# Running ranks kept in TensorE's bank, a third phase copy on VectorE, and the first lists in idle buffers

## The chip, the cores and the metric

The kernel runs on one core of one Trainium2 chip. The metric is the device time of one execution in microseconds (us), lower is better. The core has five engines with a queue each: TensorE (PE, with its weight loads shown as PEld), VectorE (DVE), ScalarE (ACT), GpSimd (POOL) and SyncE (SP, which only issues DMAs here). They run side by side and wait for each other through semaphores.

## The reference, cut to what matters

x is (128 samples, 32 channels, 512). Two layers are added onto it. The change is in the first:

```python
# layer 0: grouped conv (9 taps, 4 groups) + context, then a top-2 mixture of 8 experts
h = conv(x, weight) + (c @ c_weight.T)[:, :, None] + bias[None, :, None]
logits = h @ W_gate + b_gate                   # (128, 32, 8)
_, top_idx = top_k(logits, 2)
y_all = relu(einsum('bsd,edh->bseh', h, W_e) + b_e)
x = x + take_along_axis(y_all, top_idx[..., None], axis=2).mean(axis=2)
# layer 1: attention over 8 kernels mixes channels, then a linear layer with 4-bit weights
x = x + (einsum('boi,bih->boh', agg_w, x) + agg_b) @ dequantized_W.T + bias
```

There are 4096 tokens (sample, channel) of 512 values. The kernel doesn't compute all eight experts for each token. It sorts the tokens into lists, one region of a DRAM tensor per expert, and multiplies each list by its expert's matrix only.

## The kernel before, in words

Three stages follow each other. The order in each engine's queue is written out by hand; a step index g, s or g again runs through each stage, and every engine has its own `step1`, `step2`, `step3`.

**Stage 1** (32 steps, one per group of 4 samples, 128 tokens). For group g:
- SP has loaded x into one of four buffers `xt`. `split_phase` (L365) copies one of four phases (every fourth element) of it into a quarter of the partitions of `phases`. VectorE makes phases 0 and 1 (`split_x`, L699), ScalarE phases 2 and 3 (L573 to L578), for group g+2 while TensorE works on g+1.
- TensorE convolves (L1185 to L1190, 12 matmuls in float32, 24 records). ScalarE copies the result to `hT` (L568).
- `gate_and_rows` (L1163), one step later: four matmuls give partial gate logits and transposed rows. VectorE reduces the logits and finds the two best experts (L832 to L872); ScalarE writes the token rows to `token_list` (L596).
- `count_ranks` (L1156), two steps later: `before` (ones for every earlier token) times `chosen` gives each token's rank inside the group, `ones` times `chosen` the count per expert. VectorE adds the running offset `base` (L838), keeps `base` up to date (L848), and picks the row of each of the token's two experts (L854, L863). POOL scatters the token's row to `lists_d` twice (L522).
- In steps 16 to 26 VectorE also computes, from the counts of the first 15 groups, the table of the first eight list tiles (`early_table`, 19 instructions).
- ScalarE issues the four loads of the experts' biases `be_bc` (L603), 512 KB each, in steps 18 to 21. In steps 24 to 29 a small network for layer 1 (`mix_layers`, `mix_softmax`) is computed in between.

Steps 4 to 15 are a hardware loop (`Fori`), where waits are on computed register values; the others are written out.

**Stage 2** (71 list tiles, 128 tokens each). SP loads tile a of `lists_d` into `xt` in four DMAs and its keys in a fifth (L432, L435); before tiles 0 to 3 it waits until all 32 groups have been split out of `xt` (L424 to L426). VectorE transposes it into `lT` (`transpose_list`, L935), TensorE multiplies it by the expert's weights (`product`, L1204, four matmuls of 512 columns), VectorE adds the bias (L953), ScalarE applies the ReLU, POOL scatters the result. Tiles 0 to 3 are transposed by VectorE between its last steps of stage 1 (L961 to L969). Tiles 8 and up need the final table, which VectorE computes from the final counts (L984 to L1007) and TensorE spreads (L1248 to L1250) after product 4.

**Stage 3** (32 groups): the pairs are summed with x, mixed, and multiplied by the 4-bit matrix.

On TensorE the passage from stage 1 to 2 reads: convolution 31, ranks 29, gate 30, gate 31, product 0, ranks 30, product 1, ranks 31, three matmuls of the mixing kernels (L1150 to L1154), product 2.

## Time and profile before

| | |
|---|---|
| three runs | 516.99 us median (516.94 to 518.96) |
| the profiled execution | 518.35 us, its span 516.6 us |
| PE busy | 491.2 us (95% of the span) |
| PEld, DVE | 321.6 us (62%), 345.6 us (67%) |
| ACT, POOL | 197.6 us (38%), 157.5 us (30%) |
| mean granted TensorE clock | 0.981 of full speed |

Busy shares are means over three stages with different limits. The rows further down are read by stretch: a stretch belongs to stage 1 up to about 142 us, to stage 2 from about 152 to 395 us, to stage 3 from there. Times in a timeline row are the start in us and the duration in us; what stands in brackets is the idle time of the engine before the row and who ended it. A row with xN merges N like instructions.

### The profile page before, as it was taken

To read this page: it belongs to the slowest core of one execution; us is meant where nothing else is said; L and a number is where in the kernel's file an instruction comes from. 1 tells how busy PE (TensorE), PEld (TensorE's weight loads), DVE (VectorE), ACT (ScalarE), POOL (GpSimd) and SP (SyncE) were. 2 spreads that over 40 slices of the span, in tenths; PEclk is the share of its full clock that TensorE was granted. 3 is DMA by queue.
4 is the path that set the end of the run, shared out by engine and by line. 5 is a ranking of instruction groups with operands and counts; after the bars stand their busy time and mean duration, and the time that the engine had idled before them with its cause. 6 is when DMAs were issued, how large, how long until landed. Compare 5 with 4: busy or idle time off the path is not lost. (4 is left out here: it accounts for less than half of the span.)

```text
span 516.6 us, 10152 instructions
## 1 busy us (share of the span) xinstructions
PE 491.2 (95%) x2284; PEld 321.6 (62%) x2285; DVE 345.6 (67%) x1087; ACT 197.6 (38%) x341; POOL 157.5 (30%) x178
## 2 busy tenths in 40 slices
PE   5999999999869999999999999999997999999996
PEld 5999999989844443444444444444544777777674
DVE  6877888877546657573354435453445799999996
ACT  6798999999721111111111111111222222222220
POOL 9154555444435522233323332333224000000000
PEclk9999999999969999999999999999997999999998
DMA  6569878998467686676666657575554688889852
GB/s 182 142 233 298 285 241 269 361 374 269 154 165 188 209 228 168 165 201 181 174 187 163 183 150 197 163 191 146 155 143 169 245 292 292 277 292 287 286 184 102
DMA packets 90050, 110.94 MB, mean 215 GB/s; under 512 B 25198, under 2 KB 61726, under 8 KB 88980
## 3 DMA queue, kind: packets, MB, share of 16 engines
q1 hardware_dynamic: 71808, 69.14, 47.1%
q0 software_dynamic: 11664, 36.24, 19.7%
q10 hardware_dynamic: 6536, 5.09, 3.3%
q8 instruction: 15, 0.25, 0.2%
q14 instruction: 27, 0.22, 0.2%
HBM read 65.44 MB, written 46.51 MB: 217 GB/s over the span
## 5 line engine op out<-in xcount | busy, mean ns | idle before, releaser
L1213 PE MATMUL bank<-we,lT 128*128 x536 | 233.7, 597 | 0.7 <-DVE ring_a L953 0.7
L1213 PEld LDWEIGHTS bank<-we,lT 128*128 128x128 f32 x536 | 101.8, 191 | 128.1 <-issue 127.9
L539 POOL DMA_INDIRECT pairs_d<-ring_b,pair_i x71 | 71.0, 999 | 161.0 <-DVE pair_i L942 109.2
L630 ACT ACTIVATE ring_b<-ring_a 128x512 f32<-128x512 f32 x71 | 44.7, 630 | 196.3 <-DVE ring_a L953 188.2
L953 DVE TENSOR_TENSOR ring_a<-bank,be_bc 128x512 f32<-128x512 f32 x71 | 49.0, 691 | 101.8 <-PE bank L1213 92.4
L1187 PE MATMUL bank<-wconv,phases 128*128 128x128 f32 x768 | 93.8, 280 | 1.2 <-ACT phases L367 1.2
L522 POOL DMA_INDIRECT lists_d<-token_list,row_i x64 | 66.7, 1042 | 83.3 <-ACT token_list L596 57.1
L1187 PEld LDWEIGHTS bank<-wconv,phases 128*128 128x128 f32 x768 | 90.8, 196 | 1.4 <-ACT phases L367 1.4
L367 ACT COPY phases<-xt 32x512 f32<-32x512 f32 x64 | 71.4, 1116 | 1.2
L939 DVE STREAM_TRANSPOSE lT<-xt 128x512 f32<-128x512 f32 x71 | 49.9, 703 | 11.1 <-DMA keys<-lists_d 10.8
L367 DVE COPY phases<-xt 32x512 f32<-32x512 f32 x64 | 44.7, 698 | 10.2 <-PE bank L1187 8.5
L1174 PE MATMUL bank<-wg,lT 128*128 128x136 f32 x256 | 39.2, 298 | 4.1 <-ACT token_list L596 3.7
L1280 PE MATMUL bank<-wq,high 128*128 128x512 f32 x128 | 38.8, 426 | 3.5 <-PEq L1228 3.5
L1174 PEld LDWEIGHTS bank<-wg,lT 128*128 128x128 f32 x256 | 33.5, 198 | 5.2 <-issue 4.5
L1284 PE MATMUL bank<-wq,low 128*128 128x512 f32 x128 | 35.9, 403 | 0.0
L1259 PE MATMUL bank<-mix_bd,we 128*128 128x128 f32 x224 | 32.0, 286 | 0.0
L685 ACT CAST high<-bank 128x512 fp32r<-128x512 f32 x32 | 18.7, 586 | 34.2 <-PE bank L1259 34.2
L596 ACT ACTIVATE token_list<-bank,ctx_col 128x256 f32<-128x256 f32 x64 | 26.8, 469 | 10.9 <-DVE partial L832 9.9
L1259 PEld LDWEIGHTS bank<-mix_bd,we 128*128 128x128 f32 x224 | 27.4, 191 | 4.6 <-DVE we L1066 4.3
L1284 PEld LDWEIGHTS bank<-wq,low 128*128 128x128 f32 x128 | 24.6, 192 | 6.0
L1280 PEld LDWEIGHTS bank<-wq,high 128*128 128x128 f32 x128 | 22.7, 197 | 7.3 <-issue 4.3
L678 ACT CAST rows_r<-bank 34x128 fp32r<-34x128 f32 x32 | 8.3, 258 | 48.5 <-PE bank L1266 48.5
(196 smaller groups left out, 384.3 us busy)
## 6 DMA issues: line engine op xcount, KB each, us to landing
xt<-lists_d SPq DMA_DIRECT2D x284, 64.0 KB, 2.1
xt<-in_x SPq DMA_DIRECT2D x60, 256.0 KB, 3.9
we<-pairs_d SPq DMA_DIRECT2D x28, 512.0 KB, 4.8
we<-in_L_ffn_W_e SPq DMA_DIRECT2D x8, 1024.0 KB, 6.5
out<-orow_list SPq DMA_DIRECT2D x32, 256.0 KB, 2.8
lists_d<-orow_list SPq DMA_DIRECT2D x8, 257.0 KB
be_bc<-in_L_ffn_b_e ACTq DMA_DIRECT2D x4, 512.0 KB, 9.5
words<-pairs_d POOLq DMA_DIRECT2D x4, 512.0 KB, 5.3
```

The source lines that it names most:

```text
L367: return copy(phases[q * C:(q + 1) * C, jb, :, 1:P + 1], x_quad[jq].rearrange("c s (l q) -> c q s l", q=PH)[:, q, :, :])
L522: pool.indirect_dma_start(lists_d, bass.IndirectOffsetOnAxis(ap=row_i[:, j, k:k + 1], axis=0), token_list[:, j, :], None, bounds_check=E * ...
L539: pool.indirect_dma_start(pairs_d, bass.IndirectOffsetOnAxis(ap=pair_i[:, s % DR:s % DR + 1], axis=0), ring_b[:, s % U, :], None, bounds_c ...
L630: act.activation(ring_b[:, j, :], ring_a[:, j % 2, :], ACT.Relu, scale=0.5).then_inc(result_ready, 1)
L939: dve.transpose(lT[:, ja, :].rearrange("m (p h r) -> m h p r", p=PH, h=MH), xt[:, ja, :].rearrange("r (h p l) -> r h p l", h=MH, p=PH)).th ...
L953: dve.tensor_tensor(ring_a[:, j % 2, :], ps_exp[j % 2][:, :], be_bc[:, bass.ds(expert, 1), :].rearrange("p a n -> p (a n)"), ALU.add).then ...
L1174: mm = pe.matmul(ps_both[:, p // 2, cols], hT[:, ja % 2, p * P:(p + 1) * P], wg[:, p, :], start=True, stop=True)
L1187: mm = pe.matmul(ps_conv[j % 2][:, s * P:(s + 1) * P], phases[:, j % 2, s, t:t + P], wconv[:, t, :, :].rearrange("k p o -> k (p o)"), star ...
L1213: mm = pe.matmul(ps_exp[j % 2][:, :], lT[:, j, p * P:(p + 1) * P], we[:, bass.ds(expert, 1), p, :].rearrange("m a n -> m (a n)"), start=(p ...
L1259: mm = pe.matmul(ps_mix[a % 2][:, q * P:(q + 1) * P], y_of(a)[:, q * P:(q + 1) * P], mix_bd[:, a, :], start=True, stop=True)
L1280: pe.matmul(ps_lin[j][:, :], high[:, j % 2, q * P:(q + 1) * P], wq[:, q, :], start=(q == 0), stop=False, skip_group_check=True)
L1284: mm = pe.matmul(ps_lin[j][:, :], low[:, j % 2, q * P:(q + 1) * P], wq[:, q, :], start=False, stop=(q == PH - 1), skip_group_check=True)
```

## The change

- **Ranks.** `count_ranks` no longer restarts its bank. Before the first group, a matmul of one row puts the regions' first rows into columns 0 to 7 and zeros into 8 to 15. In each later group one more matmul (`others` times the chosen of the group before; `others` is the complement of `before`) completes the last group's contribution, so columns 0 to 7 always hold the running row number. VectorE reads it straight: `rank` and `base` additions go; the two picking instructions become one product over 2 x 8 and one reduction; the mask of both experts is made at once. VectorE's small instructions of a step go from 12 to 10. TensorE now waits until the rank of the group before was read (`picked_ready`).
- **Phases.** VectorE copies phase 2 as well (`split_third`), at the end of its step; ScalarE copies only phase 3.
- **Lists 0 to 3** are loaded into `ring_a` 0 and 1 and `ring_b` 2 and 3, idle in stage 1, with no wait for the splits. That wait now stands ahead of list 4, which also waits for the transpose of list 0.
- **Biases** are loaded in steps 0 to 3 of stage 1.
- **Order on TensorE.** 4 warm-up transposes ahead of the 12 transposes of the convolution's weights and 8 behind them; the three matmuls of the mixing kernels move ahead of gate 31.
- POOL makes `others` and `rank_init` before its other constants (four more instructions in place of one).

```diff
         ring_b = sb("ring_b", [P, U, L])
+        first_list = [ring_a[:, 0, :], ring_a[:, 1, :], ring_b[:, 2, :], ring_b[:, 3, :]]
...
+        def list_of(a, ja):
+
+            return first_list[a] if isinstance(a, int) and a < len(first_list) else xt[:, ja, :]
...
-                    if isinstance(a, int) and a < XR:
+                    if isinstance(a, int) and a == XR:
                         sp.wait_ge(act_split, NG)
                         sp.wait_ge(dve_split, NG)
-                    else:
+                    if not isinstance(a, int) or a >= XR:
                         wait(sp, lT_ready, a - XR + 1)
                         wait(sp, pair_ready, a - XR + 1)
 
                     for mh in range(MH):
-                        sp.dma_start(xt[mh * B:(mh + 1) * B, ja, :].rearrange("r (h n) -> r h n", h=MH),
+                        sp.dma_start(list_of(a, ja)[mh * B:(mh + 1) * B, :].rearrange("r (h n) -> r h n", h=MH),
...
+            pool.memset(others[:, :], 1.0).then_inc(others_one, 1)
+            pool.wait_ge(others_one, 1)
+            pool.affine_select(out=others[:, :], in_=others[:, :], compare_op=ALU.is_ge, fill=0.0, base=0,
+                               pattern=[[-1, P]], channel_multiplier=1).then_inc(consts, 1)
             exact = dict(allow_small_or_imprecise_dtypes=True)
             pool.iota(iota_e[:, :], pattern=[[1, E]], base=0, channel_multiplier=0, **exact).then_inc(consts, 1)
             pool.iota(region[:, :], pattern=[[REGION, E]], base=P, channel_multiplier=0, **exact).then_inc(consts, 1)
-            pool.iota(base[:, :], pattern=[[REGION, E]], base=P, channel_multiplier=0, **exact).then_inc(consts, 1)
+            pool.iota(rank_init[:, 0:E], pattern=[[REGION, E]], base=P, channel_multiplier=0, **exact).then_inc(consts, 1)
+            pool.memset(rank_init[:, E:], 0.0).then_inc(consts, 1)
...
-                    for q in range(PH // 2, PH):
-                        ins = split_phase(act.copy, q, ja, j % 2)
-                    ins.then_inc(act_split, 1)
+                    split_phase(act.copy, 3, ja, j % 2).then_inc(act_split, 1)
...
-                if isinstance(g, int) and hi1 + 2 <= g < hi1 + 6:
-                    e = slice((g - hi1 - 2) * 2, (g - hi1 - 2) * 2 + 2)
+                if isinstance(g, int) and 0 <= g < 4:
+                    e = slice(2 * g, 2 * g + 2)
                     act.dma_start(be_bc[:, e, :].rearrange("p e n -> p (e n)"),
                                   b_e[e].rearrange("(a e) n -> a (e n)", a=1).to_broadcast((P, 2 * L))).then_inc(be_in, 16)
...
-                for q in range(PH // 2):
-                    ins = split_phase(dve.tensor_copy, q, ja, ja % 2)
-                ins.then_inc(dve_split, 1)
+                split_phase(dve.tensor_copy, 0, ja, ja % 2)
+                split_phase(dve.tensor_copy, 1, ja, ja % 2)
+
+            def split_third(ja):
+
+                split_phase(dve.tensor_copy, 2, ja, ja % 2).then_inc(dve_split, 1)
             dve.memset(wfull[:, :, :], 0.0).then_inc(wfull_zero, 1)
             dve.wait_ge(convw_in, 16 * (C // CG))
             pick_taps(dve.tensor_copy, range(PH // 2), dve_taps)
             split_x(0, 0)
+            split_third(0)
             for t in range(SHIFTS):
                 dve.wait_ge(wT_done, t + 1)
                 dve.tensor_copy(wconv[:, t, :, :].rearrange("k p o -> k (p o)"), ps_w[t][:, 0:P]).then_inc(wconv_ready, 1)
...
                 deq_step(dve.scalar_tensor_tensor(terms_w[:, :], full_low, odd[0:RK, 0:1], full, ALU.mult, ALU.add))
             split_x(1, 1)
+            split_third(1)
             dve.wait_ge(consts, N_CONSTS)
             def context_columns():
...
                 if live(b, NG):
                     wait(dve, rank_done, b + 1)
-                    wait(dve, base_ready, b)
-                    dve.tensor_tensor(rank[:, :], ps_rank[:, 0:E], base[:, :], ALU.add).then_inc(rank_ready, 1)
+                    dve.tensor_tensor(picked[:, :, :], masks[:, :, :],
+                                      ps_rank[:, 0:E].rearrange("p (a e) -> p a e", a=1).to_broadcast((P, 2, E)), ALU.mult).then_inc(picked_ready, 1)
                 if live(a, NG):
                     wait(dve, partial_ready, a + 1)
                     if isinstance(g, int) and a == 0:
                         dve.wait_ge(gbias_ready, 2)
                     dve.tensor_tensor(logit[:, :], partial[:, :], gate_bias[:, bass.ds(a, 1), :].rearrange("p a e -> p (a e)"), ALU.add).then_inc(logit_ready, 1)
+                if live(b, NG):
+
+                    wait(dve, picked_ready, b + 1)
                 if live(a, NG):
                     wait(dve, logit_ready, a + 1)
                 if live(b, NG):
-                    wait(dve, rank_ready, b + 1)
-                    dve.tensor_tensor(base[:, :], base[:, :], ps_rank[:, E:2 * E], ALU.add).then_inc(base_ready, 1)
+                    dve.tensor_reduce(row_of[:, :], picked[:, :, :], AX.X, ALU.add).then_inc(row_ready, 1)
                 if live(a, NG):
                     dve.max(top[:, :], logit[:, :]).then_inc(top_ready, 1)
                     wait(dve, top_ready, a + 1)
                 if live(b, NG):
-                    for k in range(2):
-                        dve.scalar_tensor_tensor(picked[:, k, :], iota_e[:, :], expert_of[:, bass.ds(b, 1), 1 + k:2 + k].rearrange("p a k -> p (a k)"),
-                                                 rank[:, :], ALU.is_equal, ALU.mult,
-                                                 accum_out=row_of[:, bass.ds(b, 1), k:k + 1].rearrange("p a k -> p (a k)")).then_inc(row_ready, 1)
+                    wait(dve, row_ready, b + 1)
+                    wait(dve, scattered[jb], (b - jb) * (32 // U))
+                    dve.tensor_scalar(row_i[:, jb, :], row_of[:, :], 0.0, None, ALU.add).then_inc(rowi_ready, 1)
                 if live(a, NG):
                     dve.max_index(topi[:, :], top[:, :], logit[:, :]).then_inc(topi_ready, 1)
-                if live(b, NG):
-
-                    wait(dve, row_ready, 2 * b + 2)
-                    wait(dve, scattered[jb], (b - jb) * (32 // U))
-                    dve.tensor_scalar(row_i[:, jb, :], row_of[:, bass.ds(b, 1), :].rearrange("p a k -> p (a k)"), 0.0, None, ALU.add).then_inc(rowi_ready, 1)
-                if live(a, NG):
                     wait(dve, topi_ready, a + 1)
                     dve.tensor_scalar(expert_of[:, bass.ds(a, 1), 1:3].rearrange("p a k -> p (a k)"), topi[:, 0:2], 0.0, None, ALU.add).then_inc(expert_ready, 1)
                     wait(dve, expert_ready, a + 1)
-                    e1, e2 = (expert_of[:, bass.ds(a, 1), 1 + k:2 + k].rearrange("p a k -> p (a k)") for k in range(2))
-                    dve.tensor_scalar(chosen1[:, :], iota_e[:, :], e1, None, ALU.is_equal).then_inc(chosen1_ready, 1)
-                    wait(dve, chosen1_ready, a + 1)
+                    dve.tensor_tensor(masks[:, :, :], iota_e[:, :].rearrange("p (a e) -> p a e", a=1).to_broadcast((P, 2, E)),
+                                      expert_of[:, bass.ds(a, 1), 1:3].rearrange("p a k -> p k a").to_broadcast((P, 2, E)), ALU.is_equal).then_inc(masks_ready, 1)
+                    wait(dve, masks_ready, a + 1)
                     wait(dve, rank_done, a - 3)
-                    dve.scalar_tensor_tensor(chosen[:, ja, :], iota_e[:, :], e2, chosen1[:, :], ALU.is_equal, ALU.add).then_inc(chosen_ready, 1)
+                    dve.tensor_tensor(chosen[:, ja, :], masks[:, 0, :], masks[:, 1, :], ALU.add).then_inc(chosen_ready, 1)
+                if live(g + 2, NG):
+                    split_third((j + 2) % U)
...
-                    dve.wait_ge(base_ready, counted)
-                    early_op(dve.tensor_tensor(tint[:, :], base[:, :], region[:, :], ALU.subtract))
+                    dve.wait_ge(rank_done, counted)
+                    early_op(dve.tensor_scalar(tint[:, :], ps_rank[:, E:2 * E], 0.0, None, ALU.add))
...
+            warm_up(WARM_START // 2)
             for t in range(SHIFTS):
                 pe.wait_ge(dve_taps, t + 1)
                 pe.wait_ge(act_taps, t + 1)
                     mm = pe.transpose(ps_w[t][:, p * C:(p + 1) * C],
                                       wsel[:, t * PH + p, :, :].rearrange("o q i -> o (q i)"), ident[0:C, 0:C])
                 mm.then_inc(wT_done, 1)
+            warm_up(WARM_START)
             def context_products():
...
             def count_ranks(a, ja):
                 wait(pe, chosen_ready, a + 1)
-                wait(pe, base_ready, a)
-                pe.matmul(ps_rank[:, 0:E], before[:, :], chosen[:, ja, :], start=True, stop=True)
-                pe.matmul(ps_rank[:, E:2 * E], ones[:, :], chosen[:, ja, :], start=True, stop=True).then_inc(rank_done, 1)
+                wait(pe, picked_ready, a)
+                if isinstance(a, int) and a == counted:
+                    pe.wait_ge(early, 1)
+                if isinstance(a, int) and a == 0:
+                    pe.wait_ge(consts, N_CONSTS)
+                    pe.matmul(ps_rank[:, 0:2 * E], one_row[0:1, 0:1].to_broadcast((1, P)), rank_init[:, :], start=True, stop=False, skip_group_check=True)
+                else:
+                    pe.matmul(ps_rank[:, 0:E], others[:, :], chosen[:, (ja - 1) % U, :], start=False, stop=False, skip_group_check=True)
+                pe.matmul(ps_rank[:, 0:E], before[:, :], chosen[:, ja, :], start=False, stop=False, skip_group_check=True)
+                pe.matmul(ps_rank[:, E:2 * E], ones[:, :], chosen[:, ja, :], start=False, stop=True, skip_group_check=True).then_inc(rank_done, 1)
             def gate_and_rows(a, ja):
...
                         mm = pe.matmul(ps_low[0][0:RK, :], ones_r[:, :], wq[:, q, :], start=(q == 0), stop=(q == 3))
                     mm.then_inc(colsum_done, 1)
+            mix_layers(NG + 1 - mlp_first)
             gate_and_rows(NG - 1, (NG - 1) % U)
             pe.wait_ge(early, N_EARLY)
             pe.wait_ge(we_in, 16 * E)
...
             count_ranks(NG - 2, (NG - 2) % U)
             product(1, 1)
             count_ranks(NG - 1, (NG - 1) % U)
-            mix_layers(NG + 1 - mlp_first)
             for s in range(2, 5):
                 product(s, s % U)
             pe.wait_ge(tab_ready, 1)
```

## Rows read from the trace of the kernel before

**Rows 1.** Busy time by stretch: us, then PE, PEld, DVE, ACT, POOL; clock, DMA.
```profile
80.00:120.00 40.00, 38.21 (x337) 37.45 (x337) 32.41 (x184) 37.57 (x59) 20.50 (x20) 1.00 0.95 330
200.00:400.00 200.00, 196.46 (x476) 89.52 (x475) 98.98 (x207) 38.21 (x62) 61.87 (x64) 0.99 0.63 171
```

**Rows 2.** The page's costliest groups: ScalarE's phase copies (busy us, mean ns | idle).
```profile
L367 ACT COPY phases<-xt 32x512 f32<-32x512 f32 x64 | 71.4, 1116 | 1.2
```

**Rows 3.** Timeline of PE: convolutions 1, 4, 16, 17, 27, 30, gate 29, convolution 31.
```profile
16.29 2.92 PE L1187 MATMUL bank<-wconv,phases 128*128 128x128 f32 x24
...
27.86 2.84 PE L1187 MATMUL bank<-wconv,phases 128*128 128x128 f32 x24
...
77.19 2.84 PE L1187 MATMUL bank<-wconv,phases 128*128 128x128 f32 x24
...
81.12 2.84 PE L1187 MATMUL bank<-wconv,phases 128*128 128x128 f32 x24
...
122.83 2.92 PE L1187 MATMUL bank<-wconv,phases 128*128 128x128 f32 x24
...
136.22 2.84 PE L1187 MATMUL bank<-wconv,phases 128*128 128x128 f32 x24
...
138.95 1.17 PE L1174 MATMUL bank<-wg,lT 128*128 128x136 f32 x8
139.96 2.84 PE L1187 MATMUL bank<-wconv,phases 128*128 128x128 f32 x24
```

**Rows 4.** Timeline of VectorE: a step in the loop, one written out.
```profile
64.17 1.24 DVE L367 COPY phases<-xt 32x512 f32<-32x512 f32 x2 [0.44 <-PE bank L1187]
...
67.84 0.23 DVE L872 SCALAR_TENSOR_TENSOR chosen<-iota_e,expert_of,chosen 128x8 bf16<-128x8 f32 x1 [0.15 <-DVE chosen L869]
...
133.03 0.19 DVE L832 TENSOR_REDUCE partial<-bank 128x8 f32<-128x32 f32 x1
...
134.83 0.23 DVE L872 SCALAR_TENSOR_TENSOR chosen<-iota_e,expert_of,chosen 128x8 bf16<-128x8 f32 x1
```

**Rows 5.** Timeline at the start: a VectorE copy and the POOL memset beside it.
```profile
9.98 5.49 DVE L367 COPY phases<-xt 32x512 f32<-32x512 f32 x1
...
11.59 3.53 POOL L513 MEMSET mix_bd<- 128x4096 f32 x1
```

**Rows 6.** Timeline: a scatter's issue on POOL; two small VectorE instructions of the table.
```profile
63.87 1.04 POOL L522 DMA_INDIRECT lists_d<-token_list,row_i  x1 [1.72 <-ACT token_list L596]
...
167.37 1.27 DVE L995 TENSOR_SCALAR prefix<-late_n,block_at 128x8 f32<-128x8 f32 x1
...
170.27 0.16 DVE L1006 TENSOR_TENSOR tab_f<-row_at,used 128x1 f32<-128x1 f32 x1
```

**Rows 7.** SyncE's waits, its first list load, and VectorE's first list transpose.
```profile
SPq L426 <- DVE phases L367: 10.1, 1, 10.1
...
137.88 1.88 SPq L432 DMA_DIRECT2D xt<-lists_d  x4
...
143.78 0.71 DVE L939 STREAM_TRANSPOSE lT<-xt 128x512 f32<-128x512 f32 x1 [5.18 <-DMA keys<-lists_d]
```

**Rows 8.** Timeline of PE between stage 1 and 2, up to the table's transpose.
```profile
146.53 0.19 PE L1160 MATMUL bank<-chosen,before 128*128 128x8 bf16 x1 [3.73 <-DVE chosen L872]
...
150.10 2.15 PE L1174 MATMUL bank<-wg,lT 128*128 128x136 f32 x8 [1.32 <-ACT token_list L596]
152.04 5.29 PE L1213 MATMUL bank<-we,lT 128*128 x8
...
160.87 1.98 PE L1153 MATMUL bank<-ring_b,attT 8*128 8x512 f32 x4
...
162.92 10.57 PE L1213 MATMUL bank<-we,lT 128*128 x24
173.32 0.27 PE L1249 MATMUL bank<-ident,tab_f 128*3 128x128 f32 x1
```

**Rows 9.** PE by stretch: us, busy, granted clock, DMA share, GB/s.
```profile
152.00:154.00 2.00, 2.00 (x5) 0.50 0.76 222
```

22 lines of the change are left out of this document (12 added, 10 removed).

## The prediction

> **What bounds the kernel now.** I read the busy tenths and the windows by stretch first, then PE's timeline, then the waits of PE, VectorE and SyncE around what the change touches. In stage 2 PE alone sets the pace: it is busy 196.46 of 200 us, no other engine over 100 [rows 1]. In stage 1 PE and ScalarE are both near full, 38.2 and 37.6 of 40 us, VectorE has 32.4 [rows 1]. The reader is to see in [rows 3] that the convolutions start 4.11 us apart in the loop ((77.19 - 27.86) / 12), 4.15 us apart in steps 16 to 27 ((122.83 - 77.19) / 11) and 4.28 us apart to step 31. Where PE waits for nothing a step takes 3.93 us in the loop (77.19 to 81.12) and 3.74 us written out (136.22 to 139.96). Between the stages PE stands still for 3.73 and 1.32 us [rows 8] behind VectorE, which stood 5.18 us in its own queue for list 0 [rows 7]. Its clock had fallen by then: the granted clock is 0.50 (1.2 GHz) at 152 us [rows 9], after the idle 3.73 us, and gates 30 and 31 take 2.15 us each [rows 8] where gate 29 took 1.17 [rows 3], product 0 takes 5.3 us. What PE loses before product 2 arrives at the end one for one, as the rest of stage 2 is PE's.
>
> **Part 1, lists 0 to 3 and the order on TensorE.** SP waited 10.1 us for the splits before it issued list 0 at 137.88 [rows 7], so it was ready at 127.8. After, the eight tiles' table (done with step 26) is its last wait, and one list takes it some 3 us to issue and land (137.88 to 143.78 held the wait and the landing). List 0 is there by about 134, VectorE asks for it at about 138.6 (143.78 - 5.18): the stall goes. What is late next? List 3 is issued last, at about 137, 10 us ahead of its transpose. List 4 now waits for the splits, over by 137.8, and for list 0's transpose, so it goes out no later than it did.
> Without the stall the passage is PE's own work from convolution 31 (139.96) to product 2. At the full clock: convolution 2.68, gate 30 1.0 (138.95 to 139.96 [rows 3]), mixing kernels 2.05 (160.87 to 162.92 [rows 8]), gate 31 1.0, two products of 3.5 (10.57 / 3 [rows 8]), three counts of 0.1: 14.0 us. The mixing kernels now lie between gate 30 and 31, where PE otherwise waits about 1.2 us for ScalarE to empty gate 30's bank; they cost nothing new and cover that. Before, the same passage took 162.92 - 139.96 = 22.96. Gain 22.96 - 14.0 = 9.0; I take 8.9. Its parts: waits 5.05, the clock about 3.9 (gates 2 x 1.0, product 0 1.8). If a new wait of 3 us lets the clock fall again, the gain is 5; 9.5 is the most.
> Behind it: the final table. VectorE had it at 170.43 [rows 6], PE wanted it at 173.32 [rows 8], 2.9 us later, but 2.05 us of PE's work have moved ahead of that chain, and the POOL memset that held VectorE's instruction for 1.27 us [rows 6] comes along with the scatters. About 0.8 us is left; down to 0 and a wait of 1.5 us is in the range.
>
> **Part 2, VectorE in stage 1.** A split of two phases takes 1.24 us [rows 4], so a third adds 0.62, and I take 0.65 with its own start. The small instructions run from 65.41, the end of the copies, to 68.07 in the loop, 2.66 us for 12 (0.22 each), and from 133.03 to 135.06, 2.03 us (0.17 each), written out [rows 4]. Ten of them: 2.2 and 1.7 us. A step of VectorE is then 1.24 + 0.65 + 2.2 = 4.1 us in the loop (3.9 before) and 3.6 written out (3.3). The new forms (2 x 8 products with a PSUM operand, the reduction) aren't in the trace; taken at the spacing of those of 8 columns, at worst they save nothing (loop 4.5, written out 3.9), at best 0.15 more than said.
>
> **Part 3, ScalarE in stage 1.** It loses a copy of 1.12 us in each step [rows 2] and goes from about 3.9 to 2.8 us. So it stops pacing stage 1, and its two late table loads and the network's activations, which make steps 24 to 29 long now, fall into slack. Next in line is VectorE where it is over PE's floor, else PE.
>
> **Part 4, TensorE in stage 1.** One more bf16 matmul with 8 columns per group. From convolution 30's start to gate 29's are 2.73 us [rows 3] with the two counts in between, and 24 records of a convolution alone take 2.68 (2.84 less the end of the last one), so the two take 0.05 to 0.1. I take 0.04 for the third, floor 3.97 and 3.78; 0.1 is the upper end. The wait on `picked_ready` is met a step ahead, as VectorE reads the ranks first after the gate's reduction. Before count 15 PE waits once for the early table's first instruction, which stands behind step 16's third copy: 0 to 0.6 us.
>
> **The sum for stage 1.**
> - Loop, 12 steps: from 4.11 to 4.10, as VectorE paces: -0.1 (from -1.7 at PE's floor to +5 if the small instructions save nothing).
> - Steps 16 to 27: VectorE 11 x 3.6 = 39.9, and the early table's 19 instructions of 0.17 add 3.2: 43.1, PE's floor 42.4 with the network's matmuls; against 45.64: -2.3 (-3.5 to 0).
> - Steps 27 to 31: 17.13 now; four VectorE steps of 3.6 and some 1.9 us for the softmax with its wait for ScalarE: 16.4, so -0.7 (-1.5 to +0.5).
> - Start: a VectorE copy that began at 9.98 ended only at 15.47, when POOL's memset (11.59 to 15.12) was over [rows 5], and convolution 1 followed at 16.29. Now two copies stand behind that point in place of one (+0.65), and POOL's four instructions for one shift the memset by 0.5: +1.1. Convolution 0 may run earlier or at the full clock thanks to the 12 warm-up transposes, but then waits for the same copy. From -0.5 to +3.5 (the clock falls while PE waits some 3 us for it).
> Together -2.0.
>
> **The biases.** Four 0.5 MB loads leave steps 18 to 21, where the DMA engines are 0.95 busy [rows 1], for steps 0 to 3. x is loaded four steps ahead, and the third copy frees its buffer about 3 us later of 16, so neither makes a split wait. Nothing for the cost; the relief is inside the -2.3.
>
> **A rule that speaks against the change.** POOL issues a scatter for 1.04 us from 63.87, and two VectorE copies that start inside it, at 64.17, take their usual 1.24 us [rows 4, 6]; beside the memset a copy took 5.49 us [rows 5]. The Trainium skill (SBUF — State Buffer, on the shared port pair) has it that VectorE's fast fp32 SBUF-to-SBUF copy and GpSimd exclude each other for a whole instruction, descriptor writing included. The memsets agree with that rule, the scatters here don't.
>
> **The rivals.**
> - A, the stage 1 terms come to nothing or cost: the loop at 4.35 (+3), the start +2, and steps 16 to 31 only -2. Then 516.99 - 8.9 + 3 = 511. For: VectorE is close to being the bound. Chance 0.14.
> - B, stage 1 falls to PE's floor throughout: -1.7, -3.3, -1.5, start 0, that is -6.5 and 501.6. For: the small forms carry fewer waits. Against: the third copy alone fills VectorE's slack. Chance 0.12.
> - C, the passage gives less: a wait for the table or a fallen clock, 4 us less: 510. Chance 0.12.
> - D, slower: the third copy, at the end of VectorE's step and beside both scatters' issues, is held by them for 1.0 us each step. VectorE's step is 5.1 in the loop and 4.9 behind it: 12 x 1.0 + 15 x 0.8 + 1 = +25, less 8.9: 533. It decides from 0.4 us of hold per step (28 x 0.4 = 11). Against: [rows 4, 6]. By the skill's rule this is what would happen. Chance 0.04.
> - E, the change does not do what it says: list 0 is still late, since SP reaches it late. Then only stage 1 counts: 515. Against: SP's 10.1 us. Chance 0.03.
>
> **How the numbers follow.** The sum is -8.9 - 2.0 = -10.9, on a profiled execution of 518.35 us (span 516.6, 1.75 around it): 507.4. The median of the runs is 516.99, 1.36 less than the profiled one, so 506.1; I forecast 506.2, chance 0.55. A, B, and C lie inside 501.5 to 511.5, where I leave out D, E and the ends. 0.5% of 517 is 2.6 us, about what a measurement can tell from no change: faster by that means below 514.4. Faster 0.93, within 0.03, slower 0.04.
>
> **What would show it.** VectorE has no idle time for the keys of list 0, PE's largest wait for `chosen` is under 1 us, the clock stays at 1.00 from 140 to 160 us, and product 2 starts at about 152. ScalarE is busy about 28 of 40 us in 80 to 120, VectorE 37. Convolutions start 4.1 us apart in the loop and 3.9 behind it; convolution 1 starts at about 17.4. Wrong would be: VectorE's copies longer than 0.7 us each beside scatters, a new PE wait at the table's matmul, or stage 2 running slower than 3.4 us a tile.

## The result, and the profile after

The kernel after takes 509.11 us (median of 4 runs, 508.53 to 511.47), the kernel before 517.19 on the same chip (516.94 to 518.96): a ratio of 0.9845, 95% interval 0.9807 to 0.9883. That is 8.1 us faster, where 10.9 were forecast; inside the range. The profiled execution took 509.02 us (span 507.3), against 518.35, so the two traces differ by 9.3 us.

Busy time by stretch in the kernel after; the columns are those of [rows 1], which it answers.

```profile
80.00:120.00 40.00, 38.92 (x357) 38.12 (x356) 35.73 (x155) 28.98 (x54) 24.35 (x21) 1.00 0.89 285
200.00:400.00 200.00, 196.46 (x502) 92.88 (x502) 98.08 (x204) 39.88 (x67) 61.00 (x62) 0.98 0.63 175
```

ScalarE fell from 37.57 to 28.98 of 40 us, VectorE rose from 32.41 to 35.73, and PE rose to 38.92: in stage 1 it is now PE that is full. Stage 2 is what it was. The phase copies, from the costliest groups [rows 2]: VectorE makes 96 in place of 64, ScalarE 32.

```profile
L373 DVE COPY phases<-xt 32x512 f32<-32x512 f32 x96 | 64.1, 667 | 2.7 <-PE bank L1207 0.4
...
L373 ACT COPY phases<-xt 32x512 f32<-32x512 f32 x32 | 35.9, 1122 | 0.8
```

PE's timeline, convolution 1, then 16 and 17 [rows 3]: they start 3.90 us apart, (76.78 - 29.61) / 12 = 3.93 over the loop from convolution 4.

```profile
17.77 2.92 PE L1207 MATMUL bank<-wconv,phases 128*128 128x128 f32 x24
...
76.78 2.84 PE L1207 MATMUL bank<-wconv,phases 128*128 128x128 f32 x24
...
80.68 2.84 PE L1207 MATMUL bank<-wconv,phases 128*128 128x128 f32 x24
```

PE's timeline between the stages [rows 8]. It has no long gap any more: 0.49 us before gate 31, and the gates take 1.17, product 0 takes 3.69 us (2.15 and 5.29 before). The granted clock is 1.00 throughout 140 to 160 us, the 2.4 GHz level, where [rows 9] had 0.50. New are the waits of 0.75 us, at product 5 behind the table's transpose, and of 0.56.

```profile
140.45 1.17 PE L1194 MATMUL bank<-wg,lT 128*128 128x136 f32 x8
141.55 1.98 PE L1166 MATMUL bank<-ring_b,attT 8*128 8x512 f32 x4
...
144.16 1.16 PE L1194 MATMUL bank<-wg,lT 128*128 128x136 f32 x8 [0.49 <-ACT token_list L605]
145.27 3.69 PE L1233 MATMUL bank<-we,lT 128*128 x8
...
152.57 10.56 PE L1233 MATMUL bank<-we,lT 128*128 x24
162.97 0.27 PE L1269 MATMUL bank<-ident,tab_f 128*3 128x128 f32 x1
...
164.21 10.56 PE L1233 MATMUL bank<-we,lT 128*128 x24 [0.75 <-DVE ring_a L964]
```

SyncE issues the four lists from 125.93 us on [rows 7] (shown: the first and the last); VectorE finds list 0 landed.

```profile
125.93 2.05 SPq L438 DMA_DIRECT2D ring_a<-lists_d  x4
...
137.01 1.97 SPq L438 DMA_DIRECT2D ring_b<-lists_d  x4
```

For the experiments I use one ledger, from PE's timelines of the profiled executions. "Start" is the start of convolution 4, "loop" 4 to 16, then 16 to 27 and 27 to 31, "passage" convolution 31 to product 2, "rest" from there to the end of the span. The medians come from 4 or more runs each.

```
                        start   loop  16-27  27-31  passage   rest    median
before                  27.86  49.33  45.64  17.13   22.96  353.68   517.19
after                   29.61  47.17  44.00  16.91   14.88  354.73   509.11
lists alone             27.79  49.14  45.08  17.12   17.92  352.85   512.10
lists and order         27.79  49.09  45.39  17.13   14.30  353.80   510.37
after without lists     28.47  47.19  43.99  16.91   24.44  353.20   516.20
before with filler      27.79  49.10  45.81  17.12   20.25  355.53   514.64
third copy on ScalarE   28.50  47.77  44.71  17.03   14.13  353.16   507.97
matrix memset first     29.05  47.17  44.04  16.89   16.36  355.29   510.91
no warm-ups             29.18  47.16  43.99  16.93   14.86  355.08   509.77
rows' memset late       29.19  47.23  43.96  16.93   14.79  352.50   508.45
both memsets late       28.36  47.19  44.03  16.89   14.13  352.80   506.13
biases late             28.62  47.14  44.64  16.35   14.14  354.31   508.46
both late, third on ACT 26.30  48.32  44.71  17.00   14.13  353.44   507.97
the same, gap filled    26.71  47.90  44.75  17.00   14.13  353.31   508.79
```

One median lies within some 1 us of where another four runs would put it, since runs of one kernel spread by 2 to 5 us; differences of stretches are much sharper. The kernel before was run again beside the experiments, with medians of 517.12 (beside the first four kernels below "after"), 518.38 (third copy on ScalarE, matrix memset first, no warm-ups, rows' memset late) and 517.98 (the other four), so medians of different sets carry up to 1.3 us of that too; each ratio below is against the kernel before.

### The profile page after: what moved, and what is told of

The parts are those of the page before. It is cut to its first block and busy times, and to the rows that moved or that the text cites. A ratio compares the mean times of both kernels' runs of the same rounds, so it can differ in the third digit from the quotient of the medians.

```text
span 507.3 us, 10035 instructions
## 1 busy us (share of the span) xinstructions
PE 489.4 (96%) x2329; PEld 320.8 (63%) x2330; DVE 352.1 (69%) x992; ACT 164.7 (32%) x309; POOL 165.4 (33%) x181
## 5 line engine op out<-in xcount | busy, mean ns | idle before, releaser
L533 POOL DMA_INDIRECT lists_d<-token_list,row_i x64 | 73.4, 1147 | 67.5 <-ACT token_list L605 46.6
L373 DVE COPY phases<-xt 32x512 f32<-32x512 f32 x96 | 64.1, 667 | 2.7 <-PE bank L1207 0.4
L950 DVE STREAM_TRANSPOSE lT<-xt 128x512 f32<-128x512 f32 x67 | 47.0, 701 | 8.8 <-DMA keys<-lists_d 8.3
L1194 PE MATMUL bank<-wg,lT 128*128 128x136 f32 x256 | 37.3, 288 | 0.5 <-ACT token_list L605 0.5
L373 ACT COPY phases<-xt 32x512 f32<-32x512 f32 x32 | 35.9, 1122 | 0.8
L1194 PEld LDWEIGHTS bank<-wg,lT 128*128 128x128 f32 x256 | 31.8, 190 | 0.7 <-issue 0.6
L579 ACT COPY lT<-bank 128x512 f32<-128x512 f32 x32 | 18.7, 585 | 35.8 <-PE bank L1207 35.8
```

Source lines behind the costliest of these rows:

```text
L373: return copy(phases[q * C:(q + 1) * C, jb, :, 1:P + 1], x_quad[jq].rearrange("c s (l q) -> c q s l", q=PH)[:, q, :, :])
L533: pool.indirect_dma_start(lists_d, bass.IndirectOffsetOnAxis(ap=row_i[:, j, k:k + 1], axis=0), token_list[:, j, :], None, bounds_check=E * ...
L950: dve.transpose(lT[:, ja, :].rearrange("m (p h r) -> m h p r", p=PH, h=MH), list_of(a, ja).rearrange("r (h p l) -> r h p l", h=MH, p=PH)). ...
L1194: mm = pe.matmul(ps_both[:, p // 2, cols], hT[:, ja % 2, p * P:(p + 1) * P], wg[:, p, :], start=True, stop=True)
```

## Experiments: the lists, the order and the clock

**Lists alone.** The kernel before with lists 0 to 3 in the idle buffers and nothing else.

```diff
+        first_list = [ring_a[:, 0, :], ring_a[:, 1, :], ring_b[:, 2, :], ring_b[:, 3, :]]
...
-                    if isinstance(a, int) and a < XR:
+                    if isinstance(a, int) and a == XR:
```

> The kernel before with nothing but lists 0 to 3 in the idle buffers and their wait moved to list 4. Theory 'the stall of VectorE for list 0 cost the passage': convolution 31 starts near 140 as before, VectorE doesn't wait for list 0, the granted clock stays at 1.00, convolution 31 to product 2 takes 15.2 us (14.0 and the 1.2 that PE waits for ScalarE at gate 31) in place of 22.96: 7.7 us less, 509.5. Rival 'list 0 is late for another reason (SyncE reaches it late, or the transfer)': the stall stays, under 2 us less, 515 to 517. Rival 'the gain came from ranks and the third copy': no change.

512.10 us, ratio 0.9896 (0.9861 to 0.9932). PE's timeline of this kernel:

```profile
144.35 1.17 PE L1179 MATMUL bank<-wg,lT 128*128 128x136 f32 x8 [1.32 <-ACT token_list L601]
146.08 5.39 PE L1218 MATMUL bank<-we,lT 128*128 x8 [0.57 <-DVE lT L944]
```

And its busy time by stretch (us; PE, PEld, DVE, ACT, POOL; granted clock, DMA share, GB/s):

```profile
144.00:146.00 2.00, 1.17 (x8) 0.99 (x8) 1.86 (x13) 0.43 (x3) 0.59 (x1) 1.00 0.75 232
146.00:148.00 2.00, 1.92 (x3) 0.94 (x4) 0.00 (x0) 0.81 (x2) 1.38 (x2) 0.59 0.70 197
148.00:150.00 2.00, 2.00 (x3) 0.71 (x3) 0.00 (x0) 0.00 (x0) 0.00 (x0) 0.56 0.76 215
```

The 5.18 us stall is gone, yet PE still idles 1.32 and 0.57 us; right after it the granted clock falls towards 0.50 (1.2 GHz) and product 0 takes 5.39 us in place of 3.69. So the clock is not saved by removing the big stall alone. The expectation's 15.2 us for the passage, with the clock at 1.00, was missed by 2.7.

**Lists and order.** The same, with the mixing matmuls between gates 30 and 31.

```diff
             count_ranks(NG - 1, (NG - 1) % U)
-            mix_layers(NG + 1 - mlp_first)
...
+            mix_layers(NG + 1 - mlp_first)
             gate_and_rows(NG - 1, (NG - 1) % U)
```

> As the run with the lists alone, and the three matmuls of the mixing kernels ahead of gate 31. If they cover PE's wait for ScalarE there: 14.9 us from convolution 31 to product 2 (what the changed kernel takes), 0.3 to 1.2 us less than with the lists alone, 508.5 to 509.2. Rival 'they only push the final table's chain onto PE's path': the passage is shorter but PE waits for VectorE at product 5 by as much, and the time is that of the lists alone.

510.37 us, 0.9865 (0.9827 to 0.9902); passage 14.30, 3.6 us less than with the lists alone. The move does two things: it covers idle time, 1.89 us of it with the 0.57 behind gate 31, and with that keeps the clock (1.00 from 140 to 162 us; product 0 takes 3.60 us for 5.39). By the medians it is worth only 1.7 us, and the expected 508.5 to 509.2 was missed: "rest" grew by 0.95, and PE, which had no wait at product 5 with the lists alone, now waits 0.48 us there. So the rival in the expectation, the table's chain pushed onto PE's path, holds in part. Both small edits together give the kernel before 6.8 of the 8.1 us by the medians.

**After without the lists.** Everything of the change but the lists' buffers (the reverse of the first diff).

> The changed kernel with lists 0 to 3 in xt and the wait for the splits ahead of list 0, as before. All of stage 1's parts stay. Theory: convolution 31 starts at 137.7 (2.3 us less than before), then the stall is back, with list 0 issued some 3 us later than before since phase 2 is copied at the end of VectorE's step: 24 to 26 us from convolution 31 to product 2 or less by the 1 us of the moved matmuls, 515 to 518 in all. Rival 'stage 1 brought most of it': 511 or less.

516.20 us, 0.9983 (0.9966 to 1.0). Stage 1 is shorter (convolution 31 at 136.56 for 139.96), but this is lost in the passage, 24.44 us. VectorE's waits and PE's timeline:

```profile
DVE lT L950 <- DMA keys<-lists_d: 9.5, 5, 5.6
```

```profile
144.20 0.19 PE L1179 MATMUL bank<-chosen,others 128*128 128x8 bf16 x1 [4.81 <-DVE chosen L881]
...
144.31 2.15 PE L1194 MATMUL bank<-wg,lT 128*128 128x136 f32 x8
146.39 3.78 PE L1166 MATMUL bank<-ring_b,attT 8*128 8x512 f32 x4
```

VectorE stands 5.6 us for list 0, PE 4.81 behind it, and at the fallen clock the gate takes 2.15 and the mixing 3.78 us (1.98 at the full one). A faster stage 1 is worth little while the list is issued late.

**Before with a filler.** The kernel before, with 32 transposes of the identity where PE stands still behind VectorE.

```diff
+                if isinstance(g, int) and g == NG - 1:
+                    warm_up(32)
```

> The kernel before with 32 more transposes into an unused bank behind convolution 31, where PE stands still for 3.73 us. They compute nothing that is used. Theory 'half of the passage's loss is the clock that fell in the stall': the stall is still there in time, but the granted clock stays at 1.00, gates 30 and 31 take 1.2 us and product 0 3.7, and the time is 3 to 4 us less, 513 to 514. Rival 'the clock falls through something else, or the wait alone counts': 517 or more.

514.64 us, 0.9944 (0.9922 to 0.9966). The stall of VectorE is as before, but the filler keeps the clock through the passage:

```profile
142.50 3.66 PE L1109 MATMUL bank<-ident 128*128 128x128 f32 x32
146.84 0.18 PE L1160 MATMUL bank<-chosen,before 128*128 128x8 bf16 x1 [0.69 <-DVE chosen L872]
...
149.42 1.17 PE L1174 MATMUL bank<-wg,lT 128*128 128x136 f32 x8 [1.32 <-ACT token_list L596]
150.80 3.69 PE L1215 MATMUL bank<-we,lT 128*128 x8 [0.21 <-DVE lT L939]
```

```profile
142.00:156.00 14.00, 11.79 (x70) 8.41 (x70) 7.25 (x50) 3.41 (x10) 3.92 (x4) 1.00 0.64 166
```

The passage is 2.7 us shorter. The clock's part is larger than that, since filler and wait together take 0.6 us more than the 3.73 us of the stall, and a wait of 0.21 is new. PE's work in the passage, without filler and waits, takes 14.4 us here and 17.9 in the kernel before: 3.5 us is what the fallen clock cost.

But the clock fell later in this execution, in product 2, though PE had been busy without a pause since 150.80 us; the row of products 2 to 4 takes 12.26 us for 10.57, which is most of the 1.85 us by which "rest" grew:

```profile
160.07 12.26 PE L1215 MATMUL bank<-we,lT 128*128 x24
```

```profile
162.00:164.00 2.00, 2.00 (x4) 0.95 (x3) 0.98 (x5) 0.00 (x0) 2.00 (x2) 0.50 0.88 302
```

This execution (517.44 us, mean clock 0.987) was the slowest of the kernel's ten; the four with a mean clock of 0.994 to 0.996 took 512.92 to 513.87, 3.2 to 4.2 us under the kernel before. Why the clock fell at 161 us no run explains. The Trainium skill (TensorE: Matmul & The Clock Gate, Part 4, on PE-mode transposes) has it that a transpose doesn't count as PE-busy in the same way as other work; here 32 of them kept the granted clock at 1.00 through a stall in which it fell without them, and up to 160 us. Whether they ran in that mode the rows, which read MATMUL, don't show.

## Experiments: who paces stage 1

**Third copy on ScalarE.** The kernel after, with phase 2 split by ScalarE as before.

```diff
-                    split_phase(act.copy, 3, ja, j % 2).then_inc(act_split, 1)
+                    for q in range(PH // 2, PH):
+                        ins = split_phase(act.copy, q, ja, j % 2)
+                    ins.then_inc(act_split, 1)
...
-                if live(g + 2, NG):
-                    split_third((j + 2) % U)
```

> The changed kernel with phase 2 copied by ScalarE again; the ranks in TensorE's bank, the lists and the order on TensorE stay. Theory 'ScalarE paced the loop and the relief of ScalarE is what shortened it': the loop goes back to 4.05 to 4.1 us a step (49 us for steps 4 to 16, 47.2 in the changed kernel), steps 16 to 27 back to 45.3, and the time is 2.5 to 3 us over the changed kernel's 509.1. Rival 'the shorter chain of small VectorE instructions did it': the loop stays at 47 to 47.5 and the time at 509 or below.

507.97 us, 0.9822 (0.9781 to 0.9863): not worse than after. The busy time of its stage 1, and its group of copies on ScalarE:

```profile
80.00:120.00 40.00, 38.31 (x349) 37.68 (x348) 29.36 (x147) 38.38 (x63) 21.04 (x20) 1.00 0.86 273
```

```profile
L373 ACT COPY phases<-xt 32x512 f32<-32x512 f32 x64 | 71.5, 1117 | 1.1
```

The loop is 47.77 us with ScalarE as full as before (38.38 of 40). So of the 2.16 us that the loop lost, only 0.6 come from the copy that ScalarE gave up, and some 1.5 from the ranks: the lists, the biases and the warm-ups leave the loop as it is (49.14 against 49.33, 47.14 and 47.16 against 47.17 in the ledger). Behind the loop (16 to 27) the copy is worth another 0.7. The ranks without the third copy in an otherwise unchanged kernel before were not run, nor the third copy without the ranks, so how the two share the gain is shown from one side only; that it is VectorE's shorter chain in the ranks' edit, and not its part on TensorE, is argued.

**Biases late.** The kernel after, with the biases loaded in steps 18 to 21 again.

```diff
-                if isinstance(g, int) and 0 <= g < 4:
+                if isinstance(g, int) and hi1 + 2 <= g < hi1 + 6:
```

> The kernel after, with the four loads of the experts' biases back in steps 18 to 21 of stage 1 (before: 0.5 MB each, where the weights also come in). Prediction's theory: they cost ScalarE's queue and the DMA engines nothing that anyone waits for, so convolutions 16 to 27 stay at 44.0 us within 0.3, the start at convolution 4 within 0.5 of 29.6, and the median within 1 us of 509.1. Rival: the DMA engines are full in those steps, the loads of x come late, and 16 to 27 grows to 45 or more (part of the 1.64 us that this stretch lost came from the biases). Third theory: at the start the four loads delay the small ones (cw_sb came 1.7 us later in the profile of after), then convolution 4 is 0.5 to 1 us earlier here.

508.46 us, 0.9828 (0.9796 to 0.9860). Steps 16 to 27 grow by 0.64 us, 27 to 31 shrink by 0.56; convolution 16 to 31 is 60.99 against 60.91. So 16 to 27 misses the "within 0.3" and the rival's 45 alike, and the move of the loads is worth nothing. The third theory got its number (convolution 4 is 1.0 us earlier) but not its reason: the first bias load is issued well after `cw_sb` has landed, and other kernels with early biases had that load as early. In this execution PE waited 1.9 us for `cw_sb`, in after 3.8; over all kernels the wait is 1.8 to 2.0 us in eight profiles and 2.8 to 3.9 in six, and no edit sorts them.

## Experiments: POOL's memsets and the start

**Matrix memset first.** The kernel after, with the memset of `mix_bd` ahead of POOL's small loads.

```diff
+            pool.memset(mix_bd[:, :, :], 0.0).then_inc(mixbd_zero, 1)
             for dst, src in ((w0_sb[:, :], w0)
...
-            pool.memset(mix_bd[:, :, :], 0.0).then_inc(mixbd_zero, 1)
```

> The changed kernel with POOL's memset of mix_bd ahead of its eight small loads, at about 7.9 us, in place of behind them at 12.4. Theory 'the memset holds the copy': VectorE's copies of x for convolution 1 start at 9.5 to 11 and wait at most until about 11.5, then take 0.62 us each; convolution 1 starts where TensorE is ready, 0.5 to 1.5 us earlier than at 16.5 to 17.8, and the time is up to 1 us less. Rival 'POOL's issuing of DMAs holds it': the copy that starts at about 10 still ends only when POOL's last load is issued, 15.5 or later.

510.91 us, 0.9873 (0.9838 to 0.9907). Timelines of VectorE and of POOL in this kernel:

```profile
6.54 5.40 DVE L373 COPY phases<-xt 32x512 f32<-32x512 f32 x3
...
13.08 1.86 DVE L373 COPY phases<-xt 32x512 f32<-32x512 f32 x3
```

```profile
7.46 3.51 POOL L517 MEMSET mix_bd<- 128x4096 f32 x1
...
12.58 1.23 POOL L524 DMA_DIRECT2D b_sb<-in_L_cond_b  x2
13.80 0.63 POOL L524 DMA_DIRECT2D b_bc<-in_L_cond_b  x1
```

Three copies beside the memset need 5.40 us; three beside the issue of DMAs take 1.86, that is 0.62 each. The memset holds VectorE's fp32 copies, DMA issues don't. Convolution 4 comes 0.56 us earlier than in after, and the median is 1.8 us higher all the same. The passage came out at 16.36 us though its order of work is that of after: this time the clock fell to 0.55 behind PE's wait of 0.50 us at gate 31, and product 0 took 4.88. So the passage of after is on the edge: the kernels without warm-ups and with the rows' memset late waited 0.48 and 0.41 us there and took 3.70 us for product 0.

**No warm-ups.** The kernel after without the 12 new transposes at the start.

```diff
-            warm_up(WARM_START // 2)
...
-            warm_up(WARM_START)
```

> The changed kernel without the 4 and 8 warm-up transposes. Theory: convolution 1 waits for VectorE's third copy anyway (end 16.4 to 17.5), so convolution 0 may start 1 to 2.9 us earlier and run at half the clock, and the time moves by less than 0.5 us. Rival 'the warm-ups are worth a microsecond': the clock stays low into convolution 1, 1 to 2.5 us more.

509.77 us, 0.9852 (0.9812 to 0.9893); convolution 4 at 29.18. Convolution 0 starts and ends earlier, and convolution 1 then waits 2.06 us for VectorE's held copy. The warm-ups bring nothing and here cost nothing.

**Rows' memset late.** The kernel after, with the memset of `rows_r` behind pair tile 4 (a pair tile is a list tile of stage 2, when POOL scatters its result).

```diff
-            pool.memset(token_rows.bitcast(F32), 1.0).then_inc(mixb_one, 1)
...
+                if s == 4:
+                    pool.memset(token_rows.bitcast(F32), 1.0).then_inc(mixb_one, 1)
```

> The changed kernel with POOL's memset of rows_r behind the scatter of pair tile 4 in place of ahead of tile 0. Theory 'this memset holds the table's tensor_scalar for 1.9 us, and that is PE's wait of 0.75 us at product 5': the instruction takes 0.17 us, the table is ready 1.7 us earlier, the wait at product 5 goes, 0.5 to 0.8 us less. Rival 'another limit stands at product 5': the wait stays. Against a gain: scatters of tiles 5 to 7 start up to 3.5 us later.

508.45 us, 0.9839 (0.9786 to 0.9891). The table's instruction on VectorE that [rows 6] show, and POOL's memset, in the kernel after:

```profile
156.78 3.54 POOL L540 MEMSET rows_r<- 70x4096 f32 x1
```

```profile
158.42 1.93 DVE L1007 TENSOR_SCALAR prefix<-late_n,block_at 128x8 f32<-128x8 f32 x1
```

And the same instruction in this experiment:

```profile
157.96 0.22 DVE L1008 TENSOR_SCALAR prefix<-late_n,block_at 128x8 f32<-128x8 f32 x1
```

The instruction ended when the memset did, at 160.35 and 160.32. Without it the table is ready 1.7 us earlier, PE's waits of 0.75 and 0.56 us are gone, and "rest" falls by 2.2 us, of which these waits explain 1.3; in part the rest is the clock at the start of stage 3, which is below 1.00 from 384 to 390 us here and to 392 in after. By the medians the gain is 0.7, less than their spread.

**Both memsets late.** The kernel after, with `rows_r`'s behind pair tile 4 and `mix_bd`'s behind pair tile 7, in stage 2.

```diff
-            pool.memset(mix_bd[:, :, :], 0.0).then_inc(mixbd_zero, 1)
...
-            pool.memset(token_rows.bitcast(F32), 1.0).then_inc(mixb_one, 1)
...
+                if s in (4, 7):
+                    if s == 4:
+                        pool.memset(token_rows.bitcast(F32), 1.0).then_inc(mixb_one, 1)
+                    else:
+                        pool.memset(mix_bd[:, :, :], 0.0).then_inc(mixbd_zero, 1)
```

> The kernel after, with POOL's two large memsets taken out of the start: that of the mixing matrix (3.5 us) goes behind pair tile 7, that of the summed rows behind pair tile 4, in stage 2. Theory (the memset holds VectorE's fp32 copies): no copy of VectorE at the start takes more than 0.7 us a piece, convolution 1 starts at 13 to 14.5 us and waits for a load or PE's own work, convolution 4 at 25.5 to 27 in place of 29.2 to 29.6, and the median falls by 2 to 3 us from the kernel after, to about 506. Rival 1 (POOL's DMA issues and its scatters hold the copies, and the memset's row only lies beside them): a copy of 3 us or more stays at the start, convolution 4 stays at 29.2, and only the 0.7 us of the rows' memset is gained, 508.4. Rival 2 (the start is bound by the loads of x): the copies are short but convolutions 1 to 4 wait for DMAs, and convolution 4 comes at 28 or later.

506.13 us (505.13 to 507.13), ratio 0.9779 (0.9747 to 0.9811): the fastest version, its interval just touching that of after. The copies of VectorE run freely, and PE's waits at gate 31 and at product 5 are gone:

```profile
10.28 1.85 DVE L373 COPY phases<-xt 32x512 f32<-32x512 f32 x3
```

```profile
11.21 4.61 PE L1210 MATMUL bank<-wconv,phases 128*128 128x128 f32 x24
...
142.38 1.19 PE L1197 MATMUL bank<-wg,lT 128*128 128x136 f32 x8
143.41 3.60 PE L1236 MATMUL bank<-we,lT 128*128 x8
```

But convolution 4 comes at 28.36, not at 25.5 to 27. With the hold gone PE's own chain is on the path: the load of `cw_sb`, 12 warm-ups, convolution 0 at 4.61 us. In after the held copies had ended at 17.49 us, and convolution 1 began at 17.77 behind PE's chain, so taking away the hold alone could gain little. The load came 1 us earlier here than in after (a wait of 2.80 us for 3.76), which is most of the 1.25 us that the start lost. What the hold is worth is better seen in the next kernel, which has one copy fewer on VectorE and comes at 26.30; the load was as early there as in after without lists and in biases late, which are at 28.47 and 28.62. The same kernel without warm-ups was not run.

**Both late, third copy on ScalarE.** The diffs of both in one kernel.

> The kernel after, with the third phase copy back on ScalarE (measured alone: -1 us) and both large memsets of POOL behind pair tiles 7 and 4. If the gains add: start as in the run with both memsets late (convolution 4 at 25.5 to 27), passage 14.1, the table's instruction 0.22 us and no wait of PE at product 5, together 504.5 to 506. Rival: without VectorE's hold the start is bound by the loads or by ScalarE, which has two copies per group again, and convolution 4 comes no earlier than 28.2: 507.5.

507.97 us, 0.9816 (0.9788 to 0.9845). Convolution 4 comes at 26.30, as said, but the 2.1 us are given back by 31 (136.33 against 136.47): loop and 16 to 27 together are 1.8 us longer. The gains don't add, and ScalarE is full again (38.38 of 40 us from 80 to 120).

**The same, gap filled.** In each pair tile that is skipped at the end of stage 2 PE does ten transposes. PE also waits for the last part of the table before its loop over the tiles.

```diff
                         pe.wait_ge(lT_ready, s + 1)
+                        for _ in range(10):
+                            pe.transpose(bank[1][:, 0:P], ident[:, :], ident[:, :])
...
+            pe.wait_ge(tab_ready, 3)
```

> The same as the run with the third copy on ScalarE and both memsets late, and in each pair tile that is skipped at the end of stage 2 TensorE does 10 transposes of the identity into an idle bank, where before it stood still for 3.5 us. Theory (what differs from run to run, and 2 us of stage 3, is the clock that falls over this gap): the granted clock stays at 1.00 through the start of stage 3, the first matmuls of stage 3 take 1.17 and 1.10 us per four in place of 2.05 and 1.91, the mean granted clock of every run is over 0.995, the runs lie within 1 us of each other, and the median is 1 to 2.5 us below that of the run without them. Rival: the spread has another cause (the DMA engines, ScalarE), and the runs still spread over 3 us; or the transposes cost more in the sequencer than the clock gives back, and stage 3 starts later by 1 us.

508.79 us, 0.9834 (0.9804 to 0.9863). PE's timeline at the start of stage 3, without the filler and with it:

```profile
383.86 2.04 PE L1297 MATMUL bank<-wq,high 128*128 128x512 f32 x4 [3.55 <-PEq L1245]
385.70 1.74 PE L1301 MATMUL bank<-wq,low 128*128 128x512 f32 x4
387.27 1.05 PE L1276 MATMUL bank<-mix_bd,token_list 128*128 128x128 f32 x8
```

```profile
380.38 5.11 PE L1246 MATMUL bank<-ident 128*128 128x128 f32 x40
385.25 1.17 PE L1299 MATMUL bank<-wq,high 128*128 128x512 f32 x4
386.25 1.09 PE L1303 MATMUL bank<-wq,low 128*128 128x512 f32 x4
387.18 1.05 PE L1278 MATMUL bank<-mix_bd,token_list 128*128 128x128 f32 x8
```

The clock stays in this execution (mean 1.000 over the span), but 40 transposes are 1.4 us too long, and 0.1 us is left. The four runs still lie between 505.57 and 510.26 us. My theory that this gap's clock makes the spread was not borne out, nor quite tested: the other three runs, 508.74, 508.84 and 510.26 us, had mean clocks of 0.996, 0.996 and 0.990, so the filler did not keep the clock throughout them. The clock is a part of the spread, since in nearly every kernel the runs with the lower mean clock tend to be the slower ones, but not the whole: in two runs of the kernel without the filler it was 0.996 and the times 505.62 and 508.00. What makes the rest stays open.

## Why the forecast was right, and where it was not

By the profiled executions the 9.3 us are: up to convolution 31 -2.27 (139.96 to 137.69), passage -8.08, rest +1.05. Forecast were -2.0, -8.9 and 0, and another 1.2 us went because the profiled execution of before lay higher above its median than that of after.

- **Lists.** Right: no wait for list 0, product 2 at 152.57 for "about 152". The lists alone and the kernel without them show that they carry the gain, and that the rest of the change gives 0.9 us without them.
- **The passage.** 14.88 us for 14.0. The mixing matmuls were to cover the wait for ScalarE wholly; 0.49 us of it was left. The other 0.4 us is PE's work, 14.4 us at the full clock, which I had summed to 14.0. The lists alone show that I mis-sized what the mixing matmuls do: I counted them as cover of 1.2 us, and in the passage they were worth 3.6, 1.9 of idle time and 1.7 as they keep the clock.
- **The clock's part.** Right: said 3.9, measured 3.5, from the kernel with the filler and again from after, where PE's work in the passage takes 14.4 us for 17.9. The waits are the other 4.6 of the 8.1 (0.49 left of 5.05), for 5.05 of 8.9.
- **The loop.** This step failed: "as VectorE paces: -0.1" against -2.16, below even the -1.7 that I gave as its lowest. VectorE doesn't pace the loop, PE does, at 3.93 us a step. I took 0.22 us for each of the ten small instructions from a chain that contained waits of VectorE on itself [rows 4], which the new forms have less of. Steps of VectorE in after show it:

```profile
79.55 1.89 DVE L373 COPY phases<-xt 32x512 f32<-32x512 f32 x3
81.46 0.19 DVE L846 TENSOR_REDUCE partial<-bank 128x8 f32<-128x32 f32 x1
...
83.07 0.17 DVE L881 TENSOR_TENSOR chosen<-masks 128x8 bf16<-128x8 f32 x1
```

  From 81.46 to 83.24 are 1.78 us, written out; in the loop 1.97. With 1.89 of copies that is 3.86, under PE's 3.93, and PE has no wait in the loop at all. My step for ScalarE ("it stops pacing") named the wrong partner as well: with the copy back on it the loop is only 0.6 us longer. As far as the waits show, what paced the kernel before was the ring of gate, chain of ranks and copies, in which PE waited 1.2 us for `chosen` and VectorE 2.5 for PE. In the sum the errors cancelled in part: up to convolution 31 the change gave 2.27 us for 2.0, and that this came out so close is luck.
- **Steps 16 to 31.** -1.64 and -0.22 for -2.3 and -0.7. Right in sign, and too much each time, and the working had slips: 11 x 3.6 is 39.6, not 39.9, and 45.64 less 43.1 is 2.5, not 2.3. PE's floor that I gave for 16 to 27 was 42.4; it has a wait of 0.7 us for the early table (`tint`) there, as forecast, and what takes the rest I didn't separate.
- **The start.** +1.75 for +1.1. The hold by the memset was right, the copy that began at 11.24 ended with it at 16.23, and two more followed:

```profile
11.24 6.25 DVE L373 COPY phases<-xt 32x512 f32<-32x512 f32 x3
```

  They ended at 17.49, for the 16.1 of before (15.47 and one copy of 0.62). The memset itself came 0.77 us later than before (12.36 for 11.59), where I had said 0.5. PE came last by little, at 17.77 without a wait: `cw_sb` landed 1.7 us later in this execution (a wait of 3.8 against 2.0) and the warm-ups stand in its chain. Where the load was early (after without lists, biases late), two of the three copies passed before the hold, convolution 1 came at 16.50 and 16.65, and the start is +0.6 and +0.8.
- **The table.** "About 0.8 us is left" was wrong: the memset held the table 1.93 us, not 1.27, and a wait of 0.75 us came, as the range allowed. With the 0.56 behind it that is more than the +1.05 of "rest", for which I had forecast nothing.
- **The rule against the change.** VectorE's copies take 0.62 us each beside POOL's scatters and DMA issues, so rival D was rightly small. It is POOL that loses a little: a scatter's issue that takes 0.98 us alone takes 1.42 beside three copies, and the mean of one from 30 to 120 us is 1.16 us in after, 1.06 before and with the third copy on ScalarE. PE was not seen to wait for it.

```profile
67.68 1.90 DVE L373 COPY phases<-xt 32x512 f32<-32x512 f32 x3
```

```profile
67.75 1.42 POOL L533 DMA_INDIRECT lists_d<-token_list,row_i  x1 [1.28 <-ACT token_list L605]
```

  The Trainium skill (SBUF — State Buffer, on the shared port pair) is borne out for the memsets. For the issues it is not borne out on VectorE's side; on POOL's there is a delay, but of 0.4 us, less than the 1.90 us of the copies.

## What to carry to other kernels

Take away a stall and then look at the small gaps beside it: here 1.9 us of idle time, left over, cost another 1.7 us through the clock, and moving two microseconds of ready work into the gap took 3.6 us off the passage (1.7 off the median), where all changes of stage 1 together gave 2.3. Count a chain of small instructions without its own waits when the new form has none. Put a large memset on GpSimd where VectorE does no fp32 SBUF-to-SBUF work that anyone waits for; with both moved, the median was 3 us under the kernel after (in the profiled execution some 1 us of that is a load that landed earlier).

## What the runs showed of the hardware

- A VectorE phase copy that meets POOL's memset ends 0.3 to 0.4 us after it: from 9.98 to 15.47 with the memset's row from 11.59 to 15.12 [rows 5], from 10.07 to 15.84 with 11.97 to 15.50 (no warm-ups). It stands still before the row of the memset begins, by up to 1.9 us; no run explains that.
- At the start PE works at half speed though the row of the granted clock reads 1.00: eight warm-up transposes take 1.97 us at 1.6 us, 0.25 each, where 40 took 5.11 in stage 2, 0.13 each. Convolution 0 took 5.49 us (before), 4.72 (after), 4.61, 3.46 and 3.40 in others, convolution 1 always 2.92. With twelve more transposes ahead of it (nine kernels) convolution 0 took 3.40 to 4.77 us, without them (five) 4.34 to 5.49, so never 2.92. Its row merges 24 records, and short waits between them are not told apart from a slow clock.
- Whether the clock falls after a short idle time is not the same in each execution: 0.49 us at gate 31 left it at 1.00 in after, 0.50 us at the same place let it fall to 0.55 in the kernel with the matrix memset first, and in the kernel with the filler it fell to 0.50 at 162 us, in the midst of work.
